# Sending a mixture-of-experts layer's rows back: the sixth pair in two parts, one drain of GpSimd instead of two

## The reference, cut to what matters

```python
capacity = floor(1.25 * 4096 / 16)                  # 320 rows for each expert
top1 = argmax(gate_logits); ranks = cumsum(one_hot(top1)) - 1   # rows above the capacity are dropped
dispatch = einsum('sec,sd->ecd', sec_mask, tokens)  # tokens sorted by expert
h = gelu(einsum('ecd,edf->ecf', dispatch, w1))      # 320x128 @ 128x512, for each expert
expert_out = einsum('ecf,efd->ecd', h, w2)          # 320x512 @ 512x128
out = einsum('sec,ecd->sd', combine_weights, expert_out)        # back to the tokens' order
x = x1 + gb * out
```

## Time and profile before

| | us |
|---|---|
| median of 3 runs | 218.26 |
| the runs | 217.01, 218.26, 219.07 |
| profiled execution: span, first to last instruction | 217.0 |
| mean granted clock of TensorE, as a share of full speed | 0.967 |
| busy: TensorE / VectorE / ScalarE / GpSimd | 192.2 / 153.2 / 145.0 / 113.8 |
| expert stage: first products to the end of the program | about 134 to 217.0 |
| first send and start of the last send of GpSimd | 150.14 and 213.84 |

### The profile page before, as it was taken

One profiled execution on the slowest core, in us unless ns is written; L12 is line 12 of the kernel. 1 busy time (PEld: TensorE's weight loads), 2 busy tenths in 40 slices (PEclk: granted clock), 3 DMA queues, 4 the chain that ended last, 5 costly groups with the idle time before them and its releaser, 6 DMA issues.

```text
span 217.0 us, 4034 instructions
## 1 busy us (share of the span) xinstructions
PE 192.2 (89%) x1177; PEld 155.3 (72%) x1177; DVE 153.2 (71%) x476; ACT 145.0 (67%) x425; POOL 113.8 (52%) x139
## 2 busy tenths in 40 slices
PE   6999599999999979999988749999999999999930
PEld 4789377788879759775665414888878889788830
DVE  3657999999999999999996407156847668485430
ACT  4494868999999979987756641574855848555300
POOL 6311504431387828577767760002754378487774
PEclk9788999999999999999999996999999999999996
DMA  5999999507905013114453216999879585321000
GB/s 149 285 343 360 355 360 309 222 5 215 270 21 177 0 53 147 48 73 138 161 186 119 99 65 159 362 358 357 277 254 283 168 268 157 85 100 46 31 30 20
DMA packets 37284, 38.60 MB, mean 178 GB/s; under 512 B 2591, under 2 KB 31334, under 8 KB 37264
## 3 DMA queue, kind: packets, MB, share of 16 engines
q1 hardware_dynamic: 33936, 31.29, 46.1%
q0 software_dynamic: 3328, 7.07, 9.1%
HBM read 19.19 MB, written 18.95 MB: 176 GB/s over the span
## 4 chain that ended last, share of the span: by engine, by line
PE 59%; DVE 17%; issue 8%; POOL 7%; ACT 4%; DMA 2%; POOLq 1%; SPq 0%; DVEq 0%
PE bank L1280 14%; PE bank L1266 11%; PE bank L1039 5%; POOL out_dram L529 4%; PE bank L1083 3%; PE bank L1109 3%; PE bank L1057 3%; PE bank L1092 2%; PE bank L1078 2%; PE bank L1094 2%; PE bank L1050 2%; DVE kvsum L780 2%; PE bank L1327 2%; PE bank L1237 2%; DVE rows L804 2%
## 5 line engine op out<-in xcount | busy, mean ns | idle before, releaser
L529 POOL DMA_INDIRECT out_dram<-x_all,rest x40 | 43.2, 1080 | 42.2 <-DVE x_all L985 23.8
L503 POOL DMA_INDIRECT dispatched_rows<-rows,slot x32 | 32.2, 1006 | 16.0 <-issue 9.0
L709 ACT ACTIVATE HT<-bank 128x320 f32<-128x320 f32 x64 | 28.0, 438 | 10.2 <-PE bank L1266 9.8
L1280 PE MATMUL bank<-HT,w 128*128 128x320 f32 x112 | 32.4, 432 | 0.0
L1280 PEld LDWEIGHTS bank<-HT,w 128*128 128x128 f32 x112 | 20.6, 189 | 6.7
L1266 PE MATMUL bank<-xth,w1h 128*128 128x320 f32 x64 | 22.6, 353 | 0.2 <-DVE xtl L961 0.2
L955 DVE TENSOR_TENSOR w1l<-w,w1h 128x1024 fp32r<-128x1024 f32 x8 | 16.1, 2022 | 7.4 <-DMA dispatched_rows<-rows,slot 7.4
L1004 DVE COPY OT<-bank 128x320 f32<-128x320 f32 x14 | 6.9, 492 | 18.5 <-PE bank L1280 18.5
L1266 PE MATMUL bank<-xth,w1l 128*128 128x320 f32 x64 | 19.8, 309 | 0.0
L1266 PE MATMUL bank<-xtl,w1h 128*128 128x320 f32 x64 | 19.8, 309 | 0.0
L560 ACT ACTIVATE junk<-bank 128x128 f32<-128x128 f32 x64 | 16.5, 288 | 1.5 <-PE bank L1039 1.3
(11 more groups left out here) (172 smaller groups left out, 494.1 us busy)
## 6 DMA issues: line engine op xcount, KB each, us to landing
w<-in_L_ffn_w_dram SPq DMA_DIRECT2D x16, 512.0 KB, 7.6
dispatched_rows<-blank SPq DMA_DIRECT2D x8, 965.0 KB, 13.2
rest<-dispatched_rows SPq DMA_DIRECT2D x8, 645.0 KB, 6.4
hin<-dispatched_rows SPq DMA_DIRECT2D x7, 320.0 KB, 7.5
x_all<-in_L_attn_x_dram SPq DMA_DIRECT2D x8, 256.0 KB, 5.2
rows<-gb_row SPq DMA_DIRECT2D x8, 256.0 KB, 3.8
out_dram<-rows SPq DMA_DIRECT2D x8, 256.0 KB, 3.2
out_dram<-x_all,rest POOLq DMA_INDIRECT x40, 2.3
```

The source lines that it names most:

```text
L503: pool.indirect_dma_start(out=disp_d, out_offset=bass.IndirectOffsetOnAxis(ap=slot[:, b, j:j + 1], axis=0), in_=rows[:, b, j, :], in_offse ...
L529: pool.indirect_dma_start(out=out_d.rearrange("b t d -> (b t) d"), out_offset=bass.IndirectOffsetOnAxis(ap=rest[i % RING][:, n, C_TOK - D: ...
L709: act.activation(HT[e][:, f, :], ps_h[c % HB][:, 0:CAP], ACT.Gelu_apprx_tanh).then_inc(h_done, 1)
L1280: last = pe.matmul(ps_o[e], w2[i % RING][:, e, f, :], HT[e][:, f, :], start=(f == 0), stop=(f == NF - 1))
```

## The change

Three edits go together. `SPLIT` falls from 6 to 5, so the sixth pair's rows (i = 5) go back in two parts as the seventh's do: the transposes of its first two tiles stand inside the sixth pair behind `outer(1)`, those of the other three inside the seventh pair. `rows_back` now stands ahead of `inner(2)` in the sixth, seventh and eighth pair (before: in the seventh alone). On VectorE the split of the next pair's weights comes after the combine in the sixth and the seventh pair (before: in the seventh alone). And GpSimd is drained behind the fourth pair (i = 3) alone, no longer behind the second (i = 1).

```diff
@@ -354,7 +354,7 @@
         HEAD = CAP // P
         CUT = -(-CAP // P)
         LAST = NPAIR - 1
-        SPLIT = LAST - 1
+        SPLIT = LAST - 2
 
 
         def parts_before(i):
@@ -536,7 +536,7 @@
             for i in range(NPAIR):
                 for part, n0, n1 in parts(i):
                     send_tiles(part, i, n0, n1)
-                if i in (1, 3):
+                if i == 3:
                     pool.drain()
 
 
@@ -991,7 +991,7 @@
                 if i >= 1:
                     for part, n0, n1 in parts(i - 1):
                         combine(part, i - 1, n0, n1)
-                if i == SPLIT:
+                if SPLIT <= i < LAST:
                     w1_low(i + 1)
                 if i == LAST:
                     for part, n0, n1 in parts(i):
@@ -1302,7 +1302,7 @@
                         if hi == (n + 1) * P:
                             last.then_inc(y_ps, 1)
 
-                back = 2 if i == SPLIT else NF
+                back = 2 if i >= SPLIT else NF
                 for c in range(2 * NF - 1):
                     if c == back and i >= 1:
                         part, n0, n1 = parts(i - 1)[-1]
```

## The result

| | before | changed |
|---|---|---|
| median | 218.26 us | 216.28 us |
| lowest to highest of 22 runs | 217.01 to 219.21 | 214.37 to 218.55 |
| profiled execution: span | 217.0 | 213.9 |
| ratio of the runs, 95% interval | 1 | 0.9925, 0.9903 to 0.9948 |
| GpSimd's first send starts at | 150.14 | 148.60 |

The change is worth 0.75% (1.6 us; interval 1.1 to 2.1). The ratio compares runs in the chip's fast state alone, while the two medians, which lie 1.98 us apart, take in all runs. A reader who subtracts the two spans finds 3.1 us, and half of that is not the change's: the first send already starts 1.54 us earlier in the second profile, and nothing was changed ahead of it. That part went from +63.70 to +62.11, which is 1.59 us.

A forecast was written before the change was run, and what follows sets the result against it. Bound: GpSimd's restart after its second drain plus twenty sends. Earlier restart, cut by new idle and stretched sends, moves the last send from 213.84 to 212.35: 1.5 us off the 218.26 median gives 216.8 us, range 215.4 to 218.2.

The forecast's parts named there:

- Removed drain: GpSimd behind the second pair: without the drain, the third pair's sends start at 167.9, not 171.51, 3.6 us earlier.
- Remaining drain: GpSimd behind the fourth pair: drain holds 1.75 us, restart at 185.4 against 188.64, 3.2 us earlier.
- Stretched sends: GpSimd sends meeting VectorE's weight split: one at 185.4 loses 0.33 us, the sixth pair's sends lose 0.9.
- Rival C: GpSimd's queue needs the drain: third and fourth pairs' sends go at 2.3 us each, about 223 us; chance 0.07.
- TensorE's price: Sixth pair's transposes, split in two groups, and their wait for VectorE cost TensorE +0.37 us for all that follows.
- New bound: GpSimd runs dry before the seventh pair; its first part, send at 200.78, plus nine more starts sets the end.
- rival A: Larger gain, over 1% (2.2 us): slack ahead of the seventh pair absorbs late restarts after drains, about 215.8 us; chance 0.26.
- The rule on the port: Exclusive port lock: VectorE's add could wait up to 0.97 us for a send, saving only 0.5; left out of the sum.

The follow-up runs named there:

- The drain alone: Kernel before with only the drain behind the second pair taken out: last send starts at +62.42 us, ratio to before 0.9915 (0.9875 to 0.9956).
- the parts alone: Changed kernel with the drain behind the second pair put back: last send at +63.16 us, ratio 0.9958 (second profile); +64.49, 0.9954 (first).

## Why the prediction was right

The forecast was 216.8 us, the measured median 216.28; the saving was put at 1.5 us and is 1.59 in the stage. Of the 0.5 us between forecast and median only 0.1 is in the stage; no run tells where the rest comes from, and single runs of one kernel lie up to 4 us apart.

- **Removed drain.** Third pair's first send forecast at +17.8 (167.9), measured +17.76. Fourth: forecast +26.7, measured +26.68. Right.
- **Remaining drain.** I took 1.75 us, and it holds 180.38 + 0.97 to 176.9 + 6.5, which is 2.1; restart forecast at +35.3, measured +35.71. Here the choice of row was wrong in kind: that row was of a drain behind ten sends, this one is behind twenty, and the number turned out to matter. The restart came 0.45 us later than forecast.
- **Stretched sends.** The fifth pair's first send was forecast to lose 0.33 us to the split. It started late enough to lose nothing (184.31 + 0.97 = 185.28, the split ends at 182.35 + 2.02 = 184.37). The sixth pair lost 0.65 us and not 0.9. These two errors and the late restart cancel: GpSimd was done with the sixth pair at +48.82, forecast +48.88. That this came so close is luck; the end did not hang on it, since the gap had 1.4 us of slack.
- **Rival C** was right in one thing that it did not say. The queue does not slow down without drains, but its last drain grows. With the drain behind the fourth pair gone as well, 1.35 of the 1.59 us would have been lost in the tail. The drain that was kept costs nothing, since it stands in the slack and does work that would otherwise lengthen the end; the run without it puts the fifth pair's first send at +34.64, and it meets a weight split at once (1.92 us).
- **TensorE's price.** Forecast 0.37 us on the seventh pair's first part, measured 49.74 - 49.44 = 0.30; the wait itself 0.36, measured 0.33. Eighth pair's last tile: forecast 0.73 later, measured 207.90 - 148.60 = 59.30 against 58.72, so 0.58. It was in time, as forecast.
- **New bound.** Gap ahead of the seventh pair forecast 1 to 2 us, measured 1.74; first send forecast at +50.64, measured +50.56; last +62.2, measured +62.11. The run with one send less shows that this is the bound.
- **Not separated in the prediction:** what each edit is worth alone. The drain alone gives 1.28 us, the parts alone 0.54, together 1.59. They overlap, since both only bring GpSimd to the seventh pair earlier, and TensorE sets when that may start.
- **Wrong, without harm:** that the span is all the time of an execution, and that the profiled one is the fast end of the runs. In the 252 later runs 1.7 to 3.1 us lie around the span (215.92 against 213.9 in the changed kernel's). From this I estimate that the execution with a span of 217.0 took 218.7 to 220.1 us, so it was not at the fast end. The saving was taken from the median, so nothing hung on it, except rival A, which rested on it: in the two profiles of before the restart behind the second drain is the same within 0.01 us, and their difference of 1.9 us arises ahead of the stage. So nothing that was measured supports A.
- **The rule on the port.** The two-input adds that begin during a send kept their 0.42 us. One of the eighth pair's took 0.35 in place of 0.29; it begins at 202.95, 0.03 us ahead of a send. This is nothing near the 0.97 that the rule of the Trainium skill (page "SBUF — State Buffer", section on the two separate sides) would allow for. What the same page (section on who interferes with whom) calls inferred, that a `tensor_tensor` does not disturb descriptor generation, does not carry over to these indirect sends: they end 0.80 us behind the subtraction, wherever that is put. Which part of a send is held up no run tells; it also reads its row numbers from SBUF (`rest`).

## What to carry to other kernels

Where a queue of sends ends a kernel, find the last part at which it runs dry: work before that is free, work behind it counts in full, and leaving out one send on either side tells which is which. A step that only tidies up (a drain) belongs into such slack; taking it out altogether may lengthen the last one. When two engines interfere, the order of one of them decides which of the other's instructions is hit, so move the long instruction before counting a gain.

## What the runs showed of the hardware

- A drain of GpSimd is longer the more indirect DMAs have gone since the last: held 1.6 to 1.75 us with 10, 1.9 to 2.2 with 20, 3.3 with 40, 4.3 with 52; 2.7 with 32 that have all landed. With 10 it ends 0.4 to 0.5 us behind the last landing, also where weight loads make that landing late (4.8 to 5.4 us held).
- An indirect send that starts inside a VectorE subtraction of two SBUF operands ends 0.80 us behind that instruction, and one that starts inside an add of two SBUF operands 0.85 us behind it, where its own 0.97 us would not last longer. One that starts 0.08 us earlier (162.82, with the split at 162.90, in before) keeps its 0.97 us.
- A send that starts up to 0.04 us behind the beginning of such an add also keeps its 0.97 us (9 cases), and the add takes 0.03 to 0.07 us longer (0.35 in place of 0.29 at 202.95 in the changed kernel).
- GpSimd restarts 0.8 to 0.9 us behind the end of a drain, and 0.8 behind the signal that rows are ready.
